# Start of a fused attention and expert kernel: one rounding handed to Pool, products, projections and norms in another order

## The reference

```python
x = x + xattn(layernorm(x), ctx_2048)    # both quant-dequantised, block of 128 (weight: 128x128)
hidden = layernorm(x)
h = rmsnorm(hidden, attn_norm_w)
q, k, v = (h @ w.T for w in (q_w, k_w, v_w))       # heads of 128: 16, 4, 4
q = apply_rope(rmsnorm(q, q_norm_w)); k = apply_rope(rmsnorm(k, k_norm_w))
attn = softmax(causal(q @ k.T / sqrt(128))) @ v
hidden = hidden + attn @ o_w.T
probs = softmax(rmsnorm(hidden) @ gate_w.T)        # top 2 of 8 experts
return x + hidden + sum(topw * (silu(t @ wg.T) * (t @ wu.T)) @ wd.T)
```

## Time and profile before

| | |
|---|---|
| median of 3 runs | 1435.12 us (1435.06, 1435.12, 1441.99) |
| profiled execution, its own time | 1443.74 us |
| its span | 1441.9 us |
| mean granted clock of TensorE | 0.953 |
| busy PE, DVE, ACT, POOL | 1271.6, 843.9, 719.3, 382.5 us |
| first maxima of scores start at | 93.94 us |

### The profile page before, as it was taken

How to read it: one execution, slowest core, us unless ns; L and a number is a source line. 1 busy time by engine, 2 the same in 40 slices (tenths; PEclk the granted TensorE clock), 3 DMA queues, 4 the chain that set the end, 5 groups by cost and what they waited for, 6 DMA issues and landing times. The chain is left out here.

```text
span 1441.9 us, 22860 instructions
## 1 busy us (share of the span) xinstructions
PE 1271.6 (88%) x6845; PEld 1026.0 (71%) x6845; DVE 843.9 (59%) x2480; ACT 719.3 (50%) x2290; POOL 382.5 (27%) x545
## 2 busy tenths in 40 slices
PE   1867899999999989979999899998999399999995
PEld 0455767787776767757767787786767289998895
DVE  7667876666886665568767566665543523223231
ACT  6447655555675556466655556554453122233331
POOL 0223121232322222222213132331310223334332
PEclk9888999999999999989999999999999599999998
DMA  3270325441455465627544754765301887887432
GB/s 96 76 274 23 119 101 176 168 163 50 165 147 169 169 195 177 234 93 224 173 163 149 232 179 159 203 220 181 113 23 59 257 316 209 257 242 208 77 61 37
DMA packets 89894, 228.50 MB, mean 158 GB/s; under 512 B 12272, under 2 KB 50032, under 8 KB 79536
## 3 DMA queue, kind: packets, MB, share of 16 engines
q1 hardware_dynamic: 77536, 201.86, 40.0%
q0 software_dynamic: 10848, 24.71, 9.2%
q10 hardware_dynamic: 1392, 0.47, 0.2%
HBM read 146.76 MB, written 80.24 MB: 157 GB/s over the span
## 5 line engine op out<-in xcount | busy, mean ns | idle before, releaser
L537 POOL TENSOR_TENSOR prob<-prob,rtotal 128x128 f32<-128x128 f32 (+2 forms) x192 | 117.0, 614 | 463.1 <-DVE rtotal L1283 436.9
L1277 DVE TENSOR_SCALAR_CACHE_REDUCE prob<-bank,nscale 128x128 f32<-128x128 f32 (+3 forms) x256 | 134.9, 544 | 167.4 <-PE bank L715 167.1
L954 ACT ACTIVATE prob<-prob,bias 128x128 f32<-128x128 f32 (+3 forms) x256 | 144.8, 566 | 155.4 <-DVE prob L1277 154.4
L679 PE MATMUL bank<-w_hi,hT_hi 128*128 128x512 f32 x480 | 175.1, 365 | 15.4 <-DVE rot L1242 15.3
L734 PE MATMUL bank<-pT,v 128*128 128x512 f32 (+3 forms) x512 | 177.2, 448 | 9.4 <-ACT pT L960 8.7
L960 ACT ACTIVATE pT<-bank 128x512 f32<-128x512 f32 (+3 forms) x256 | 104.0, 434 | 140.4 <-PE bank L723 139.8
L679 PE MATMUL bank<-w_hi,hT_lo 128*128 128x512 f32 x480 | 163.4, 340 | 0.0
L679 PE MATMUL bank<-w_lo,hT_hi 128*128 128x512 f32 x480 | 163.3, 340 | 0.0
L1587 PE MATMUL gu<-we,xT_hi 128*128 x624 | 156.9, 333 | 3.5 <-DVE xT_lo L1703 2.7
L514 POOL TENSOR_TENSOR r<-r,rot 128x640 f32<-128x640 f32 x60 | 99.8, 1663 | 188.8 <-DVE rot L1242 188.8
L713 PE MATMUL bank<-kT_hi,qT_hi 128*128 128x128 f32 (+3 forms) x256 | 103.8, 405 | 15.7 <-DVE prob L1277 15.6
(11 more groups left out here) (312 smaller groups left out, 2862.9 us busy)
## 6 DMA issues: line engine op xcount, KB each, us to landing
w_hi<-ws_scratch SPq DMA_DIRECT2D x24, 1024.0 KB, 5.1
w_lo<-ws_scratch SPq DMA_DIRECT2D x24, 1024.0 KB, 7.5
we<-wx_scratch SPq DMA_DIRECT2D x16, 1408.0 KB
we<-wx_scratch SPq DMA_DIRECT2D x16, 768.0 KB
stage<-in_wexp SPq DMA_DIRECT2D x64, 176.0 KB, 2.4
wx_scratch<-ehi SPq DMA_DIRECT2D x64, 176.0 KB, 2.6
wx_scratch<-stage SPq DMA_DIRECT2D x64, 176.0 KB, 2.6
stage<-in_wqkvo SPq DMA_DIRECT2D x40, 256.0 KB, 3.2
```

Of the source, the lines that this page charges most:

```text
L537: nc.gpsimd.tensor_tensor(p, p, rtotal[:, 4 * h + q:4 * h + q + 1].broadcast_to([P, KEYS[q]]), ALU.mult).then_inc(prob_ready, 1)
L679: last = nc.tensor.matmul(o, hT[a][:, k, t * P:(t + 1) * P], wkv(j, c, k) if kv else wq(j, c, k), start=(k == 0 and n == 0), stop=(k == KC ...
L954: nc.scalar.activation(p, p, ACT.Exp, bias=bias[:, 4 * h + q:4 * h + q + 1], scale=-1.0, accum_out=total[:, 4 * h + q:4 * h + q + 1]).then ...
L1277: nc.vector.tensor_scalar(prob[(G * it + h) % (LAG + 1)][:, P_AT[q]:P_AT[q] + KEYS[q]], bank[SC + q % 2][:, 0:KEYS[q]], nscale[it % 2][:, ...
```

## The change

It touches the part ahead of the loop.

1. Pool scales the four context chunks, one instruction a chunk (in1 is `cinv`, broadcast over 128 columns), ahead of its tables. ScalarE did it with four instructions a chunk.
2. VectorE rounds rows 0 and 1, chunk 0, rows 2 and 3, chunks 1 to 3. Before: rows 0 to 3, chunks 0 to 3.
3. TensorE does the product of chunk 0 tile by tile between the row transposes; chunks 1 to 3 follow as before. ScalarE's order is fitted to it.
4. All six pieces of the first weights are split ahead of the additions, and SP fetches pieces 6 to 8 (group 1) ahead of the save of x1.
5. `hidden_norm` comes before `lo_h`.
6. Keys and values are projected ahead of the queries; the keys' norm is computed by itself (`first_norms(G, G + 1)`), and their transposes stand before the last query tile's projection. The queries' norm follows, without `start_norms`.

```diff
             nc.gpsimd.memset(n15[:, :], 1.5).then_inc(pool_own, 1)
+            pool.wait_ge(cinv_ready, 1)
+            for k in range(KC):
+                blocks = cb[:, k, :].rearrange("p (n d) -> p n d", d=P)
+                nc.gpsimd.tensor_tensor(blocks, blocks, cinv[:, k * TT:(k + 1) * TT].unsqueeze(2).broadcast_to([P, TT, P]), ALU.mult).then_inc(cv_ready, 1)
             tables()
             for t in range(TT):
+                add_rope(0, t)
+            for t in range(TT):
                 add_first(t)
-            for t in range(TT):
-                add_rope(0, t)
...
+            first_product(0, 0)
+            first_product(0, 1)
+            transposes_x(0, 2)
+            first_product(0, 2)
+            transposes_x(0, 3)
+            first_product(0, 3)
+            for k in range(1, KC):
+                for t in range(TT):
+                    first_product(k, t)
...
             for t in range(TT):
+                project(0, t, True)
+            for t in range(TT - 1):
                 project(0, t, False)
-            for t in range(TT):
-                project(0, t, True)
-            for i in range(G):
+            transpose_qk(0, 0)
+            project(0, TT - 1, False)
+            for i in range(1, G):
                 transpose_qk(0, i)
...
-            for t in range(TT):
-                scale_ctx(0, t)
-                dequantise_rows(0, t)
-                if t:
-                    copy_xT(0, t - 1)
-            copy_xT(0, TT - 1)
+            dequantise_rows(0, 0)
+            dequantise_rows(0, 1)
+            copy_xT(0, 0)
+            dequantise_ctx(0, 0)
+            copy_xT(0, 1)
+            dequantise_rows(0, 2)
+            copy_xT(0, 2)
+            dequantise_rows(0, 3)
             act.wait_ge(const_in, 16 * 6)
             nc.scalar.activation(identb[:, :], ident[:, :], ACT.Copy)
-            dequantise_ctx(0, 0)
+            copy_xT(0, 3)
+            dequantise_ctx(0, 1)
             hi_qkv(0, 0)
...
-            for c in range(RING_W):
+            for c in range(QKV):
                 lo_qkv(0, c)
             for t in range(TT):
                 add_product(0, t)
             sum_norm(0)
-            lo_qkv(0, 3)
+            hidden_norm(0)
             for t in range(TT):
                 lo_h(0, t)
...
             for t in range(TT):
+                rest_kv(0, t)
+            first_norms(G, G + 1)
+            first_keys()
+            for t in range(TT):
                 rotate(0, t, False)
                 lo_qkv(1, t)
-            for t in range(TT):
-                rest_kv(0, t)
-            start_norms(0)
-            first_norms()
-            apply_norms(0)
-            for i in range(G):
+            first_norms(0, G)
+            first_scale()
+            lo_qk(0, 0)
+            for i in range(1, G):
                 lo_qk(0, i)
```

More of the change, by code:

```diff
@@ L434, in _ @@
                 load_raw(n)
+            for n in range(QKV, QKV + RING_W):
+                load_raw(n)
             save_x1(0)
-            for n in range(QKV, 2 * QKV):
+            for n in range(QKV + RING_W, 2 * QKV):
                 load_raw(n)
@@ L604, in first_maxima, with first_product @@
                 nc.tensor.transpose(bank[PV][:, P:P + NB], cmb[:, :], ident[0:NB, 0:NB]).then_inc(cm_back, 1)
-            def first_products():
-                for k in range(KC):
-                    pe.wait_ge(cd_ready, k + 1)
-                    for t in range(TT):
[L610 to L614, removed]
+            def first_product(k, t):
+                pe.wait_ge(cd_ready, k + 1)
+                if k == 0:
+                    pe.wait_ge(xT_ready, t + 1)
+                last = nc.tensor.matmul(bank[FIRST_P[t]][:, :], r[:, t, k * P:(k + 1) * P], cb[:, k, :], start=(k == 0), stop=(k == KC - 1))
+                if k == KC - 1:
+                    last.then_inc(xp_done, 1)
             def transposes_h(f, t):
@@ L673, in project @@
                     need(pe, o_added, TT * (j - 2))
-                if j == 0 and not kv:
+                if j == 0 and kv:
                     pe.wait_ge(x1_ready, TT)
@@ L1007, in _ @@
                 hi_qkv(1, t)
-            for t in range(TT):
-                square_kv(0, t)
+            hi_qk(0, 0)
             hi_qkv(1, 4)
             hi_qkv(1, 5)
-            for i in range(G):
+            for i in range(1, G):
                 hi_qk(0, i)
@@ L1317, in _ @@
             ctx_scales(0)
-            for t in range(TT):
-                round_rows(0, t)
-            for k in range(KC):
+            round_rows(0, 0)
+            round_rows(0, 1)
+            round_ctx(0, 0)
+            round_rows(0, 2)
+            round_rows(0, 3)
+            for k in range(1, KC):
                 round_ctx(0, k)
             dve.wait_ge(const_in, 16 * 6)
-            for c in range(RING_W):
+            for c in range(QKV):
                 lo_qkv(0, c)
@@ L1327, in _ @@
             sum_norm(0)
-            lo_qkv(0, 3)
+            hidden_norm(0)
             for t in range(TT):
                 lo_h(0, t)
-            hidden_norm(0)
-            lo_qkv(0, 4)
-            lo_qkv(0, 5)
             dve.wait_ge(table_in, 16 * 3)
```

41 lines of the change are left out of this document (26 added, 15 removed).

## The result

| | median, us | lowest to highest | executions |
|---|---|---|---|
| before, same chip | 1437.71 | 1434.27 to 1445.46 | 10 |
| after | 1442.76 | 1440.52 to 1449.27 | 10 |

The ratio is 1.0041, with a 95% interval of 1.0022 to 1.0059: slower, by 5 us, and just outside the forecast range. The profiled execution took 1442.49 us with a span of 1440.7, at a mean granted clock of 0.953. The profiled execution of before was one of its slower ones (1443.74), so the two traces are equally long, and a comparison of these two alone would find nothing.

A forecast was written before the change was run, and what follows sets the result against it. TensorE was taken as the bound, with work for 88% of the span; the change touched only the serial start-up. Terms +1.6 - 1.4 - 0.4 = -0.2 us, put on the 1435.12 median, gave 1435.0 us; range 1429 to 1442.

The forecast's parts named there:

- Rounding, +4.6 us: Start-up rounding on VectorE: four Pool products each hold it 1.15 us, so it ends near 43.4 us.
- Pool's own work: Time of one Pool 128x512 scaling product, taken as 1.15 us from an earlier addition, bounds 0.72 to 1.71.
- Products, no gain: TensorE's context products before the additions: first tile's done at 49.8 us, no gain against 50.05.
- weights ahead of the additions: VectorE's six low parts of first weights precede the first addition, moving it from 50.05 to 51.7 us, +1.6.
- (a): Rival: Pool's holds cost VectorE nothing, rounding ends at 38.8, total 1431 us; chance 0.15.
- (b): Rival: Pool's chained instructions, eight tables, keep VectorE out; first addition at 53.8, total 1437 us; chance 0.2.
- (c): Rival: Pool must load code before its first product, as in a 5.84 us idle seen later; total 1436 us; chance 0.05.
- Projections -1.4: TensorE's start-up projections, keys first, shrink from 19.8 to 18.4 us; bounds -2.5 to 0.
- tail -0.4: Last projection to first score maxima: 11.1 us instead of 11.5, as keys finish early; bounds -1.4 to +0.5.
- a shift passes to the end one to one: From the first maxima both kernels run the same instructions, so a start shift reaches the end fully, barring a transfer wait.
- My sign of being wrong: Stretch after 95 us changing by over 3 us; also last rounding near 39, or low parts waiting 4 us or more.
- two levels: Executions of the kernel before taken to fall at 1435 or 1442 us; the upper level ended the range.

The follow-up runs named there:

- pool_only: Parts 1 to 3 alone put into the kernel before, with keys, norms and weight ring unchanged; median 1441.19 us, ratio 1.0043.
- before_prompt: Kernel before, but SyncE fetches expert-weight piece m + 2 instead of m + 3 behind piece m's saves (the early fetch); median 1423.39 us, ratio 0.9895.
- no_keys_first: Changed kernel with part 6 undone (queries projected first, one norm for all heads); median 1439.76 us, ratio 1.0019.
- after_padded: Changed kernel with 16 one-column copies added in ScalarE's early idle time; median 1441.16 us, ratio 1.0014.
- after_again2: Changed kernel run once more without an edit; median 1444.18 us, ratio 1.0052 against the kernel before.
- keys_and_weights: Kernel before with parts 4 to 6 only, without Pool's scaling and the new rounding and product order; median 1437.52 us, ratio 1.0003.
- before_again: Kernel before, unchanged, run again; median 1436.35 us, ratio 1.0001.
- before_padded: Kernel before with 16 one-column copies added on ScalarE at the start; median 1436.59 us, ratio 0.999.
- after_prompt: Changed kernel with SyncE fetching expert-weight piece m + 2 instead of m + 3 behind piece m's saves; median 1425.94 us, ratio 0.9915.
- the second group: Repeats with the early fetch (piece m + 2 instead of m + 3): kernel before 1423.28 us, changed kernel 1423.82 us; parts 1 to 3 and 4 to 6 separately.

## Why the prediction was wrong, step by step

- **Rounding, +4.6 us (end at 43.4).** The mechanism was right, the size too large: +2.7, the end at 41.51. The term that was mis-sized is Pool's own work: I took 1.15 us from its addition in the earlier trace rows, and each hold was 0.66 to 0.72. Why this product needs less than that addition is not shown.
- **Products, no gain; weights ahead of the additions, first addition +1.6.** The addition starts at 49.89: -0.16. VectorE did come to it behind a low part of weights, as forecast, but 1.8 earlier, since rounding ended 1.9 earlier than forecast. "No gain" for the products was wrong: the first tile's was done at 47.3, not 49.8, and in pool_only, without the weights in front, the addition starts at 47.95, 2.1 ahead of before. So the products gained some 2 us, and the weights in front took them back.
- **Rivals (a) to (c).** (a) falls: the holds cost something. (b) falls: Pool's tables, 0.72 alone, show 0.90 to 1.19 beside low parts, and the five low parts take 0.87 each; neither starves the other. (c) falls: the first product starts at 19.39, with no gap.
- **Projections -1.4, tail -0.4.** Sum -1.8 from a first addition at 51.7. From 49.89 the measured stretch to the maxima is 43.94, before 43.89: no gain in this execution. The projections run from 62.47 to 81.98, 19.5 us, so they gave -0.3 and not -1.4; my sum for them also held a slip (48 matmuls at 0.22 are 10.6, not 10.9). The tail from there took 11.85, +0.4 and not -0.4. The effects that I named are there (no wait of TensorE for `k_ready`; ahead of kT's low part VectorE is idle for 0.24 instead of the 1.82 of the earlier trace rows), but TensorE stands 4.40 us for Pool's addition instead, and from 85.7 us on it is granted 1.2 GHz for 13.7 us, before for 6.8: the clock of the first 160 us is 0.85 against 0.88. Other traces of the changed kernel have the maxima at 93.15, and with edits that leave the start alone at 92.23, 92.33 and 94.05; the mean of these five is 93.1, that of five traces with before's start 94.1. So -0.2 was right for this execution by luck (-0.16 and +0.05 where I had +1.6 and -1.8), and 0.8 us short on the mean: the start gained more than I forecast.
- **The step that failed** is the one behind the sum: "From there I take both kernels to run the same instructions ... a shift passes to the end one to one, unless a wait on a transfer takes part of it." The instructions are the same, and up to 500 us the traces are too. Behind it ScalarE waits in line for saves that stand behind weight loads, and a shift of 1 or 2 us of the start changed the mean by 4 to 6. With SP's wait taken away by before_prompt and its companions, 4 of the 6 us are gone: that the loss comes mainly through it is shown. My own words named the exception, a wait on a transfer; I did not look for one behind 115 us. My sign of being wrong, a stretch after 95 us that changes by more than 3 us, shows in the medians alone: between the two profiled executions it changes by 1.1.
- **The forecast's spread.** I had three executions of before, 1435.06, 1435.12 and 1441.99, and read two levels. There are none: 99 executions fill 1431 to 1447, with a mean of 1437.5. A median of three was 2.4 us low, which alone is a third of the miss of 7.8.

**What stays open.** Why a start that is earlier or level makes these waits dearer in the mean. With the old fetch the medians of all six kernels that have parts 1 to 3 lie above before (by 2 us in no_keys_first and after_padded to 7 in after_again2, three of the six intervals with no change inside), and that of keys_and_weights, without them, does not. The save that stands behind an instruction packet at about 895 us splits the traces in the same way and is worth 1.1 to 2.7 us there; it is the best lead, and untested. The sums of the waits don't tell it: ScalarE's waits for `ehi` come to 20.3, 11.9 and 14.3 us in before, before_again and before_padded, to 17.3, 16.2 and 20.9 in after, after_again2 and after_padded. And these waits are not all that parts executions. Behind the last mile post, where no piece is staged any more, nine traces take 361.3 to 361.9 us with 43 to 46 us at 1.2 GHz, seven take 363.4 to 365.5 with 49 to 52, with either fetch. The 1.7 us that remain with the early fetch may be the clock: in after_prompt's trace two steps of 1.5 and 2.5 us, at 284 and 352 us, are stretches at 1.2 GHz that before_prompt does not have there. That is read from single traces, not tested. In after_prompt ScalarE also waits 2.6 us for fetched pieces (`stage`), in before_prompt 0.5, in both traces of the second group 0.

## What to carry to other kernels

Before a shift is passed on one to one, look through the whole trace for in-order waits on DMA landings in the critical engines' streams; where there are some, the kernel turns a shift into noise of several us, and a mean can move against the sign of the shift. A queue that waits for the landing of the save it has just issued is such a place: let it wait for the one before. And take the scatter away first: with it gone, six executions (standard deviation about 2 us) gave a mean as sure as some twenty had before (3.5 us).

## What the runs showed of the hardware

- VectorE and Pool, both with SBUF operands, take turns: beside Pool's 128x512 product with a broadcast factor (1.3 us recorded each, in a row of four), one instruction of VectorE was stretched by 0.66 to 0.72 us, and Pool's 128x256 ones went from 0.72 to 0.90 to 1.19 beside VectorE's low parts. In the rows of one meeting only, as the earlier trace rows, the stretch had been up to 1.2 us. The Trainium skill ("SBUF — State Buffer", section "SBUF: two separate sides") has a lock held for a whole instruction; the trace agrees with it, if Pool's instruction is taken as the 0.75 us that are left when its own wait is taken off (an estimate). A recorded duration holds the wait, so it is not the price: here that was about half of it.
- A 176 KB save issued at 894.5 us landed 1.8 us later in before_again and 4.1 us later in no_keys_first. In the second, eight of its 128 packets ran only behind a 16 KB packet of the instruction queue that ended at 897.24 us. Such a packet comes every 16 to 35 us between 500 and 1000 us (20 or 21 in the ten traces with the old fetch).
- The same idle of TensorE, 2.3 us in two parts around 222 us, was followed by 2.4 GHz in after and by 1.2 GHz in after_again2, the same program.
